# Null keys' values taken out of the attention's matmuls and added once a sequence

## The reference

```python
nkv = null_kv.reshape(HEADS, NUM_NULL_KV, 2, DIM_HEAD)
k = jnp.concatenate([nk, k], axis=2)
v = jnp.concatenate([nv, v], axis=2)
q = _l2norm(q) * q_scale
k = _l2norm(k) * k_scale
sim = jnp.einsum('bhid,bhjd->bhij', q, k) * ATTN_SCALE
...
sim = jnp.where(causal_mask[None, None], neg, sim)
attn = jax.nn.softmax(sim, axis=-1)
out = jnp.einsum('bhij,bhjd->bhid', attn, v)
out = out.transpose(0, 2, 1, 3).reshape(b, n, HEADS * DIM_HEAD)
return out @ w_out
```

## Time and profile before

| what | value |
|---|---|
| time, median of 3 | 2685.38 us (2684.07 to 2686.55) |
| profiled execution | 2686.31 us, its span 2684.7 us |
| busy over the span | TensorE 90%, VectorE 62%, ScalarE 56%, GpSimd 53% |
| mean granted TensorE clock | 0.966 |
| first stage | from the start to about 832 us |

### The profile page before, as it was taken

One profiled execution on the slowest core, in us unless ns is written; L12 is line 12 of the kernel. 1 busy time (PEld: TensorE's weight loads), 2 busy tenths in 40 slices (PEclk: granted clock), 3 DMA queues, 4 the chain that ended last, 5 costly groups with the idle time before them and its releaser, 6 DMA issues. The chain is left out here.

```text
span 2684.7 us, 62902 instructions
## 1 busy us (share of the span) xinstructions
PE 2409.9 (90%) x24633; PEld 1880.2 (70%) x24633; DVE 1672.1 (62%) x4392; ACT 1495.1 (56%) x3193; POOL 1425.4 (53%) x2261
## 2 busy tenths in 40 slices
PE   3999999999997688887999899999999776788887
PEld 3888888888885455556777777777777666455555
DVE  4677777777765567764544466666666521566656
ACT  3666666666663367764444466556666432466664
POOL 4778787787876644433433244444444412655544
PEclk9999999999998789999999999999999988899998
DMA  3691000000000100000000000000000054000000
GB/s 112 216 327 62 2 2 2 2 2 2 2 2 1 32 21 2 2 2 12 11 1 1 3 4 6 5 4 6 6 6 4 12 170 129 17 7 8 4 1 32
DMA packets 23255, 83.14 MB, mean 31 GB/s; under 512 B 4113, under 2 KB 11026, under 8 KB 21938
## 3 DMA queue, kind: packets, MB, share of 16 engines
q1 hardware_dynamic: 19810, 71.90, 8.4%
q0 software_dynamic: 3152, 7.21, 0.9%
HBM read 71.89 MB, written 46.79 MB: 44 GB/s over the span
## 5 line engine op out<-in xcount | busy, mean ns | idle before, releaser
L826 POOL TENSOR_TENSOR XR<-XR,T 128x256 f32<-128x256 f32 x512 | 375.4, 733 | 429.8 <-DVE T L709 399.7
L590 ACT ACTIVATE P<-ps 128x384 f32<-128x384 f32 (+1 forms) x512 | 250.7, 542 | 164.8 <-PE ps L2399 164.8
L2399 PE MATMUL ps<-P,V 128*64 128x256 f32 (+3 forms) x4096 | 333.4, 347 | 2.1 <-ACT P L590 2.1
L1190 ACT ACTIVATE P<-ps 128x768 f32<-128x768 f32 x256 | 207.9, 813 | 149.1 <-PE ps L2399 149.1
L1262 DVE TENSOR_REDUCE qa<-ps 128x2 fp32r<-128x512 f32 x256 | 176.7, 690 | 163.4 <-PE ps L2399 162.7
L2399 PEld LDWEIGHTS ps<-P,V 128*64 128x64 f32 (+1 forms) x4096 | 185.7, 123 | 101.2 <-issue 6.3
L2399 PE MATMUL ps<-mk,identb 128*128 128x256 bf16 (+1 forms) x1024 | 196.5, 294 | 59.0 <-DVE qa L1263 56.7
L720 DVE TENSOR_REDUCE sm<-ps 128x2 f32<-128x512 f32 (+1 forms) x256 | 130.8, 552 | 179.4 <-PE ps L2399 178.4
L1352 POOL TENSOR_SCALAR_AFFINE_SELECT P<-P 128x512 f32<-128x512 f32 x256 | 162.7, 635 | 137.8 <-ACT P L1190 137.7
L837 POOL TENSOR_TENSOR ss<-ss,nhalf 128x16 f32<-128x16 f32 x64 | 187.7, 2933 | 5.3
L2394 PE MATMUL ps<-wA,zT 128*128 128x256 f32 (+1 forms) x544 | 170.6, 314 | 3.6 <-DVE T L709 2.2
(11 more groups left out here) (320 smaller groups left out, 7268.0 us busy)
## 6 DMA issues: line engine op xcount, KB each, us to landing
rows_i<-in_zero SPq DMA_DIRECT2D x16, 1208.0 KB, 32.9
rows_o<-in_zero SPq DMA_DIRECT2D x16, 1208.0 KB, 82.1
w<-in_m_w SPq DMA_DIRECT2D x23, 578.0 KB, 4.0
zt<-rows_i SPq DMA_DIRECT2D x23, 128.0 KB, 3.1
rows_o<-yo POOLq DMA_DIRECT2D x23, 128.0 KB, 3.8
stg<-in_t_w SPq DMA_DIRECT2D x11, 256.0 KB, 2.7
XR<-in_x SPq DMA_DIRECT2D x4, 512.0 KB, 8.5
out<-XR SPq DMA_DIRECT2D x8, 256.0 KB, 2.0
```

Of the source, the lines that this page charges most:

```text
L590: e.activation(self.P[at % 6][:, :], K.ps.ap("st", s, g, h)[:, 0:self.w], ACT.Exp, bias=0.0, scale=1.0 if kind == 0 else 0.125).then_inc(K ...
L826: p = po.e.tensor_tensor(x, x, self.T[g % 2][:, par, pr], ALU.add)
L1190: e.activation(self.P[(2 * g + n) % 6][:, :, 0:384], K.ps.ap("st", s, g, n)[:, :, 0:384], ACT.Exp, bias=0.0, scale=self.scale).then_inc(K. ...
L2399: return self.te.matmul(o, l, r, start=start, stop=True, skip_group_check=True)
```

## The change

The null weights no longer go through the transposed attention. What is done instead:

- Null scores stand in head order (t, head, n), so `dve_null` needs two instructions for four. GpSimd adds the two null exponentials of each head (L875 in the new file), and VectorE adds that to the softmax sums before the reciprocal.
- At part out, GpSimd multiplies the null exponentials with the reciprocals into pn, which holds 64 weights (2 tiles x 16 heads x 2) for the 128 tokens of a partition set.
- Once a sequence a new item "null" of three parts starts at the tick after the last unit's out: TensorE transposes pn (128x64) and ScalarE copies it to pnT; TensorE multiplies with nvw (64x256, float32); VectorE adds the result to XR. `done` of the sequence is that add.
- nvw, null values times w_out, is made on the chip once: eight float32 matmuls from a staged 128x512 array in unit (0, 0) at part 8, and two copies on ScalarE. nvs, nvo and their preparation go.
- kb's pieces are loaded first, then the null values.

```diff
             for u in range(4):
                 items.append((16 * b + first + 4 * u, 1, "unit", (b, u), unit))
+            if kind == 0:
+                items.append((16 * b + first + 12 + unit, 2, "null", (b,), 3))
...
+        if name == "null":
+            return 3 if k == 0 else 2
...
+    def pe_nvw(self, pe):
+        K, n = self.K, self.nvs_at
+        ps = K.ps.take(pe, self.G, "nvw")
+        K.staged(pe, n)
+        for j in range(8):
+            p = pe.e.matmul(ps[0:64, 0:128], K.stg[n % 2][:, 64 * j:64 * j + 64], K.wO[:, 128 * j:128 * j + 128],
+                            start=j == 0, stop=j == 7)
+        p.then_inc(K.ps.full_of("nvw"), 1)
+    def pe_null(self, pe, b, k):
+        K, s = self.K, self.s
+        if k == 0:
+            ps = K.ps.take(pe, self.G, "pnT", s, b)
+            pe.wait_ge(self.shared, 4 * b + 4)
+            K.tr(ps[0:64, 0:128], self.pn[b % 2][:, :]).then_inc(K.ps.full_of("pnT", s, b), 1)
+        if k == 1:
+            ps = K.ps.take(pe, self.G, "nul", s, b)
+            pe.wait_ge(self.nvs_in, 1)
+            pe.wait_ge(*K.ps.read("nvw"))
+            pe.wait_ge(*K.ps.read("pnT", s, b))
+            K.acc(ps[:, 0:256], self.pnT[b % 2][:, :], self.nvw[:, :], start=True).then_inc(K.ps.full_of("nul", s, b), 1)
...
                 p = K.tr(ps[:, 128 * i:128 * i + 128], fv(nm[:, i, :]))
-            if kind == 0:
-                pe.wait_ge(self.pnull, g + 1)
-                for i in range(2):
-                    p = K.tr(ps[0:96, 256 + 128 * i:384 + 128 * i], fv(self.pn[g % 2][:, i, :]))
...
-        if kind == 0:
-            pe.wait_ge(self.nvs_in, 4)
-            pe.wait_ge(*K.ps.read("mT", s, g))
-            for pr in range(2):
-                c = 256 * u + 128 * pr
-                K.acc(pv[:, 256 * pr:256 * pr + 256], self.nvs[:, 0, c:c + 128], self.pnT[g % 2][:, :], start=pr == 0)
-            K.acc(sm[:, 0:256], self.nvo[:, 4 * u:4 * u + 4, :].rearrange("p h c -> p (h c)"), self.pnT[g % 2][:, :],
-                  start=True)
...
+                if k == 2:
+                    b = a[0]
+                    xs = K.XR[:, 2 * b:2 * b + 2, :].rearrange("p t c -> p (t c)")
+                    dv.wait_ge(self.summed, 4 * b + 4)
+                    dv.wait_ge(*K.ps.filled("nul", self.s, b))
+                    e.tensor_tensor(xs, K.ps.ap("nul", self.s, b)[:, 0:256], xs, ALU.add).then_inc(
+                        K.ps.out_of("nul", self.s, b), 1)
...
         if self.part("sT", k) is not None:
+            rs, sums = self.rs[g % 2], K.ps.ap("sT", s, g)[:, 0:256].rearrange("p (a c) -> p a c", c=32)[:, :, 0]
+            if kind == 0:
+                if g >= 2:
+                    dv.wait_ge(self.shared, g - 1)
+                dv.wait_ge(self.pnull, g + 1)
             dv.wait_ge(*K.ps.filled("sT", s, g))
-            e.reciprocal(self.rs[g % 2][:, :], K.ps.ap("sT", s, g)[:, 0:256].rearrange("p (a c) -> p a c", c=32)[:, :, 0]
-                         ).then_inc(K.ps.out_of("sT", s, g), 1)
+            if kind == 0:
+                dv.after(dv.step(e.tensor_tensor(rs[:, :], sums, self.sm[g % 4][:, 48:56], ALU.add)))
+            e.reciprocal(rs[:, :], rs[:, :] if kind == 0 else sums).then_inc(K.ps.out_of("sT", s, g), 1)
...
         if k == self.tk["mx"] + 3:
-            sm, pn = self.sm[g % 4], self.pn[g % 2]
+            sm = self.sm[g % 4]
             po.wait_ge(self.rec, g + 1)
-            if g >= 2:
-                po.wait_ge(*K.ps.filled("mT", s, g - 2))
-            po.wait_ge(K.pn_in, 2)
-            s6 = sm[:, 32:48].rearrange("p (t a) -> p t a", t=2)
-            d = po.step(e.tensor_copy(pn[:, :, 0:8], s6))
-            e.tensor_copy(pn[:, :, 64:72], s6)
-            po.after(d)
-            e.tensor_tensor(pn[:, :, 32:40], s6, fv(pn[:, :, 0:8]), ALU.subtract).then_inc(self.pnull, 1)
+            ex = sm[:, 32:48].rearrange("p (a n) -> p a n", n=2)
+            e.tensor_tensor(sm[:, 48:56], ex[:, :, 0], ex[:, :, 1], ALU.add).then_inc(self.pnull, 1)
+        if k == self.tk["out"]:
+            b, u = g // 4, g % 4
+            sm, ex = self.sm[g % 4], self.sm[g % 4][:, 32:48].rearrange("p (t h n) -> p t h n", t=2, n=2)
+            if b >= 2 and u == 0:
+                po.wait_ge(*K.ps.filled("pnT", s, b - 2))
+            po.wait_ge(*K.ps.read("sT", s, g))
+            e.tensor_tensor(
+                self.pn[b % 2][:, :].rearrange("p (t h n) -> p t h n", t=2, n=2)[:, :, 4 * u:4 * u + 4, :], ex,
+                self.rs[g % 2][:, :].rearrange("p (t h) -> p t h", t=2).unsqueeze(3).to_broadcast([128, 2, 4, 2]),
+                ALU.mult).then_inc(self.shared, 1)
```

More of the change, by code:

```diff
@@ L181, in __init__ @@
             self.sn = [sb(f"sn{s}_{i}", [128, 64], F32) for i in range(2)]
[L182 to L185, removed]
+            self.pn = [sb(f"pn{s}_{i}", [128, 64], F32) for i in range(2)]
+            self.pnT = [sb(f"pnT{s}_{i}", [64, 128], F32) for i in range(2)]
+            self.nvw = sb(f"nvw{s}", [64, 256], F32)
             self.on = sb(f"on{s}", [128, 128], F32R)
@@ L198, in done @@
     def done(self, b):
-        return self.summed, 4 * b + 4
+        return self.K.ps.read("nul", self.s, b) if self.kind == 0 else (self.summed, 4 * b + 4)
     def number(self):
         if self.kind == 0:
-            self.nvs_at = self.K.chunks(self.nvs_in, 3)
-        self.kb_at = self.K.chunks(self.kb_in, 5 if self.kind == 0 else 1)
+            self.kb_at = self.K.chunks(self.kb_in, 5)
+            self.nvs_at = self.K.chunks(self.nvs_in, 1)
+        else:
+            self.kb_at = self.K.chunks(self.kb_in, 1)
     def zi(self, b, i):
@@ L242, in pe @@
                 a[0].pe(pe, a[1], k)
+            elif name == "null":
+                self.pe_null(pe, *a, k)
             elif name == "unit":
+                if self.kind == 0 and a == (0, 0) and k == 8:
+                    self.pe_nvw(pe)
                 self.pe_unit(pe, *a, k)
+    def pe_nvw(self, pe):
[18 more added lines that the diff above has]
+            K.acc(ps[:, 0:256], self.pnT[b % 2][:, :], self.nvw[:, :], start=True).then_inc(K.ps.full_of("nul", s, b), 1)
     def pe_beff(self, pe):
@@ L460, in pe_pv @@
                     p = K.acc(pv[64 * par:64 * par + 64, 256 * pr + q:256 * pr + q + w], V[:, kt, 2 * pr + par, :],
-                              P[2 * pr + par][:, c:c + w], start=kind == 2 and kt == 0 and pr == 0)
+                              P[2 * pr + par][:, c:c + w], start=kt == 0 and pr == 0)
         p.then_inc(K.ps.full_of("pv", s, g), 1)
@@ L465, in pe_pv @@
                 p = K.acc(sm[32 * h:32 * h + 32, q:q + w], self.one[:, 0:32], P[h][:, c:c + w],
-                          start=kind == 2 and kt == 0)
+                          start=kt == 0)
         p.then_inc(K.ps.full_of("sm", s, g), 1)
@@ L492, in act @@
                 a[0].act(ac, a[1], k)
+            elif name == "null":
+                if k == 0:
+                    b = a[0]
+                    if b >= 2:
+                        ac.wait_ge(*self.K.ps.filled("nul", self.s, b - 2))
+                    ac.wait_ge(*self.K.ps.filled("pnT", self.s, b))
+                    ac.e.activation(self.pnT[b % 2][:, :], self.K.ps.ap("pnT", self.s, b)[0:64, 0:128], ACT.Copy).then_inc(
+                        self.K.ps.out_of("pnT", self.s, b), 1)
             elif name == "unit":
@@ L495, in act @@
                     self.act_kb(ac)
+                if self.kind == 0 and a == (0, 0) and k == 8:
+                    self.act_nvw(ac)
                 self.act_unit(ac, *a, k)
@@ L512, in act_kb, with act_nvw @@
             e.activation(o, i, ACT.Copy).then_inc(self.kb_in, 1)
+    def act_nvw(self, ac):
+        K = self.K
+        ac.wait_ge(self.nv_zero, 1)
+        ac.wait_ge(*K.ps.filled("nvw"))
+        for t in range(2):
+            r = slice(32 * t, 32 * t + 32)
+            i = ac.e.activation(self.nvw[r, 128 * t:128 * t + 128], K.ps.ap("nvw")[r, 0:128], ACT.Copy)
+            i.then_inc(*((K.ps.out_of("nvw"), 1) if t else (self.nvs_in, 1)))
     def act_prep(self, ac, b, k):
@@ L570, in act_unit @@
             if g >= 4:
[L571 removed]
+                ac.wait_ge(self.shared, g - 3)
             ac.wait_ge(self.nul, g + 1)
@@ L616, in dve @@
                 a[0].dve(dv, a[1], k)
+            elif name == "null":
+                if k == 2:
+                    b = a[0]
+                    xs = K.XR[:, 2 * b:2 * b + 2, :].rearrange("p t c -> p (t c)")
[3 more added lines that the diff above has]
+                        K.ps.out_of("nul", self.s, b), 1)
             elif name == "unit":
-                if self.kind == 0 and a == (0, 0) and k == 0:
-                    self.dve_nvs(dv)
                 self.dve_unit(dv, *a, k)
@@ L771, in dve_null @@
             dv.wait_ge(self.rec, g - 3)
-        for t in range(2):
-            d = dv.step(e.tensor_tensor(sn[:, t], snr[:, t], rq[:, t].to_broadcast([128, 2, 2, 2]), ALU.mult))
-        dv.after(d)
-        for t in range(2):
```

(7 more changed lines are left out.)

53 lines of the change are left out of this document (15 added, 38 removed).

## The result

The changed kernel takes 2694.89 us (median of 10 runs, 2689.69 to 2701.58) against 2686.68 (10 runs, 2683.99 to 2689.32) of the kernel before on the same chip: ratio 1.0032, 95% interval 1.0022 to 1.0042, so it is slower by 8.2 us. I had forecast 2689, range 2668 to 2702, with slower as the likeliest by a hair.

The account below looks back on a forecast made before the run. The prediction took TensorE's queue, busy 96.00 of 96 us, to bound the first stage. Its terms, -43.5 + 12 + 21 + 13 + 0.5 = +3 us, gave 2689 us, range 2668 to 2702.

Parts of the forecast that it names:

- A: First stage, TensorE: removed pn transposes and null matmuls save 0.68 us in each of 64 units, -43.5 us.
- B: First stage, TensorE: one added transpose and one float32 matmul, 0.75 us, 16 times, +12 us.
- C: First stage: masks wait for the PSUM bank until VectorE adds nul into XR, 1.40 us in 15 sequences, +21 us.
- D: First stage: GpSimd's chain makes TensorE wait ahead of raw's transposes, 0.6 and 0.25 us, 15 times, +13 us.
- TensorE hardly waited there: First stage, mT's transposes: no longer waiting for pnull was to change nothing.
- a seam at P,V: TensorE, change of matmul kind at P,V: a seam of 0.1 us may stay, paid before and after, so it cancels.
- four passes: Added float32 matmul: true FP32 makes four passes through the array; four times nvs's 0.11 would be 0.44 us.
- Rival 1: PSUM ring doesn't bite, the masks' wait ends early: 2668 us, chance 0.11.
- if the waits fall elsewhere: Sign in the profile after: TensorE waiting anywhere but ahead of masks for the add and ahead of raw's transposes means forecast wrong.
- Rivals 2 and 3: GpSimd doesn't bind, 2676 us, chance 0.10; first stage follows TensorE's instructions alone, 2654 us, chance 0.07.
- Rival 4: GpSimd's two new small steps take 0.6 us each, not 0.3, ahead of raw: 2698 us, chance 0.20.
- Small terms: First stage: other engines' changes nothing; at its end the next stage waits for VectorE's add, +0.5 us.

Follow-up runs that it names:

- the add first: Changed kernel with VectorE's add of nul into XR put first in its tick, ahead of the mx and ss reductions: 2673.72 us, 0.9956 of before.
- The run without null values: Changed kernel with its null item left out, so the output lacks the null keys' values while their weights still count in the softmax sum: 2663.30 us.
- earlier preparation: Changed kernel with each first-stage sequence's preparation two ticks earlier: 2703.27 us; with the add first as well, 2684.13 us.

## Why the forecast came out, step by step

The sum, in us a sequence, against the period of +0.73:

| term | forecast | measured |
|---|---|---|
| A, removed from TensorE, 4 units | -2.72 | -2.28 |
| B, null transpose and matmul | +0.75 | +0.83 |
| C, masks wait for the add | +1.40 | +1.38 |
| D, GpSimd's chain | +0.85 | +0.98 |
| before's own small losses, gone | 0 | -0.19 |
| sum | +0.28 | +0.72 |

A is read from the normal unit and taken four times, B from the rows below, C from the period with the add first, D from the masks' place. The last term is what before itself lost: 0.10 for KL, which D's 0.98 contains, and 0.09 for pn's transposes, which are gone. The forecast had the latter at nothing ("TensorE hardly waited there").

**A is the step that was mis-sized.** 0.57 a unit, exactly the lower bound, instead of 0.68: 7 us in 64 units, as much as the whole difference between 2689 and 2694.89 (the other misses nearly cancel). I had booked a seam at P,V as one that "cancels". It does not: raw's second group now runs straight into P,V and takes 0.53 (345.05 to 345.58), not the 0.35 that it takes ahead of pnT. The removed instructions, counted from start to start, took 0.75 us, and the unit got 0.57 shorter: the rest is the seam of the new neighbours, which before's trace does not show.

**B** is at its upper bound: from the last wA matmul 0.21 to the product, 0.63 for it, and 0.12 of that was there anyway (0.72); the transpose of pn makes the way from raw's second group to P,V 0.11 longer (0.64 us, 320.53 to 321.17, against 0.53). 0.83, or 13.3 us instead of 12. The run without null values gives 0.86. On the prediction's sentence about four passes: float32 took 0.31 us more than float32r to the follower, close to three more passes at nvs's 0.11, so the rows agree with it.

**C** was right in place, mechanism and size: 1.38 measured, 1.40 forecast, the add 0.41 us, where zT's row gave 0.47. The run with the add first shows its worth, 21.2 us. Rival 1 is out.

**D** came out near in size (0.98, forecast 0.85) but in another place and for the most part by another mechanism; that the sizes agree is luck. The prediction itself had named "if the waits fall elsewhere" as a sign of being wrong. It had GpSimd's chain, tied to wO two units earlier, arrive late at raw's transposes. What happened lies within one tick: z waits for GpSimd's statistics, KL is queued behind z on VectorE, and the masks wait for KL's bank. I had followed GpSimd into the tiles that TensorE reads from it, and not through VectorE. And I had taken 96.00 us busy of 96.00 for no wait, where the masks stood 0.09 us late already. Of the growth from 0.09 to 0.98, 0.59 is TensorE's own shorter stretch and 0.29 GpSimd's hold on z. At raw's transposes, the forecast's place, 0.64 us is left; without the 0.98 lost ahead of them that would be a wait of about 0.34 (an estimate, 0.98 less 0.64), and not 0.85. With VectorE's order moved (earlier preparation) a wait at raw does appear. Rivals 2 and 3 are out: both waits are there.

**Rival 4** failed on its price: GpSimd's two new steps take 0.20 and 0.22 us, not 0.6. Its time, 2698, lies nearer to the measured 2694.89 than the forecast's 2689 does; only the rows tell them apart. The result is slower by C and D on a smaller A.

**Small terms.** The head got 1.1 us shorter (z's first transposes stand at 60.68, before at 61.83), within my 2. At the end the add runs behind the last sum, ahead of the next stage's work:

```profile
841.13 0.42 DVE L662 TENSOR_TENSOR XR<-ps,XR 128x256 f32<-128x256 f32 x1 [2.70 <-POOL XR L854]
```

Its 0.42 is the 0.5 forecast. From z's first transposes to z's last in this stage (738.70, now 747.52) the loss grows from -1.1 to +8.8 us; behind them it stays, +8.6 at the last sum.

## What to carry to other kernels

Where TensorE is busy throughout and its work is cut, take each tile that it waits for and compare two lengths from the last point at which both engines meet: TensorE's own work, and the other engines' chain, through all the queues on its way. Here the chain (GpSimd's statistics, z, KL, a bank) had no slack at all, while the direct hand-over of raw had 0.8 us. A small distance between one engine's end and TensorE's start is not slack: compare it with the distance in a real wait (0.15 us here), and TensorE's start with its normal spacing. In this kernel the instruction that frees a PSUM bank belonged at the front of its tick: moving one add ahead of reductions that wait for TensorE's later work turned +8 us into -12. A control on the kernel before is needed for a helpful edit where it can be made, since two of mine moved the time there too.

## What the runs showed that I had not expected

- VectorE's small operations took longer beside GpSimd's work: z on two tiles took 0.7 us in two rows of 0.35 where GpSimd had small steps, and 1.41 and 1.55 beside its sum; nm on 128x8 took 0.17, and 0.59 to 0.72 in before and up to 1.03 with the earlier preparation beside raw's products. An order that put z beside the sum lost what it gained.
- A power of GpSimd costs nearly the same on one column (0.58) as on two (0.71); on 16 columns it takes 2.92 to 2.94.
- A product in float32 with 256 columns took 0.63 us to its follower, in float32r 0.32.
- The view of waits books 0.16 us less than a stalled TensorE loses here, and losses of 0.12 us and less not at all: before's 0.19 a sequence was in no list.
